# A hybrid layer on one Trainium2 core: weight loads moved to another queue, row statistics split by batch, one Newton step fewer, and the next batch's transposes moved ahead of the output product

## The reference, cut to what matters

```python
def _layernorm(x, axis=-1, eps=1e-05):
    m = jnp.mean(x, axis=axis, keepdims=True)
    v = jnp.var(x, axis=axis, keepdims=True)
    return (x - m) / jnp.sqrt(v + eps)
...
    q = elu(xn @ Wq + bq) + 1; k = elu(xn @ Wk + bk) + 1; v = xn @ Wv + bv      # 16 heads of 16
    kv = jnp.einsum('bkhd,bkhm->bhdm', k, v)
    out = jnp.einsum('bqhd,bhdm->bqhm', q, kv)
    normalizer = jnp.einsum('bqhd,bkhd->bqh', q, k)
    out = out / jnp.maximum(normalizer, 1e-6)[..., None]
    return out.reshape(B, S, D) @ Wo + bo
...
x = x + attention(layernorm(x))      # the layer that the change is about
x = x + ffn(layernorm(x))            # 8 experts, each token goes to one
x = x + mamba(layernorm(x))          # causal convolution, selective scan, gate
x = x + ffn(layernorm(x))
```

## Time and profile before

| what | value |
|---|---|
| median of 3 runs | 1615.09 us (1612.84 to 1615.52) |
| the profiled execution | 1617.17 us |
| its span, first to last instruction | 1615.4 us |
| mean granted TensorE clock | 0.918 of full speed |
| busy: PE, DVE, ACT, POOL | 1385.1, 1063.7, 952.1, 916.6 us |

### The profile page before, as it was taken

The page is one execution under the profiler, slowest core; times in us unless marked ns, Lnnn a source line. Parts: engine busy times, 40 slices in busy tenths (PEclk is TensorE's granted clock), DMA queues, the critical chain, the costliest instruction groups (busy, mean ns, idle before and its releaser), DMA issues.

```text
span 1615.4 us, 22069 instructions
## 1 busy us (share of the span) xinstructions
PE 1385.1 (86%) x6934; PEld 979.2 (61%) x6934; DVE 1063.7 (66%) x1625; ACT 952.1 (59%) x1749; POOL 916.6 (57%) x417
## 2 busy tenths in 40 slices
PE   2899878799997998989989899999997652949997
PEld 1566576799843555555655556555565541938997
DVE  5566546233341798999899998899989983362332
ACT  1222121343324899998998989989899870203442
POOL 1111000455300799889989899898998984004552
PEclk9999968899998999999999999999998685568999
DMA  9100021667430494894958949579496793316663
GB/s 301 50 26 26 27 78 52 206 207 211 117 104 14 100 225 107 194 206 110 223 131 196 221 111 222 139 175 217 101 225 156 161 222 104 126 40 193 207 208 95
DMA packets 98196, 235.66 MB, mean 146 GB/s; under 512 B 10601, under 2 KB 41454, under 8 KB 85552
## 3 DMA queue, kind: packets, MB, share of 16 engines
q0 software_dynamic: 21376, 119.30, 33.8%
q1 hardware_dynamic: 72496, 111.42, 22.7%
q10 hardware_dynamic: 4224, 3.67, 0.7%
HBM read 116.65 MB, written 18.88 MB: 84 GB/s over the span
## 4 chain that ended last, share of the span: by engine, by line
PE 62%; ACT 11%; DVE 11%; issue 8%; POOL 4%; DMA 2%; SPq 1%; ACTq 1%; POOLq 0%; DVEq 0%
PE ps L1110 11%; PE ps L1334 10%; PE ps L1265 9%; PE ps L1274 8%; ACT arena L630 4%; ACT arena L640 4%; PE ps L1363 4%; DVE arena L1058 4%; PE ps L1135 3%; PE ps L1303 3%; POOL arena L423 2%; PE ps L1405 2%; PE ps L1172 2%; PE ps L1126 2%; PE ps L1208 2%
## 5 line engine op out<-in xcount | busy, mean ns | idle before, releaser
L1110 PEld LDWEIGHTS ps<-cst,arena 128*128 128x128 f32 x2524 | 330.8, 152 | 364.0 <-issue 234.2
L423 POOL TENSOR_TENSOR arena<-arena 128x2048 f32<-128x2048 f32 x98 | 463.0, 4726 | 117.9 <-DVE arena L1058 87.9
L1110 PE MATMUL ps<-cst,arena 128*128 128x128 f32 x2524 | 410.2, 293 | 119.4 <-ACT arena L640 49.3
L1058 DVE TENSOR_TENSOR_SCAN arena<-arena,ps 128x512 f32<-128x512 f32 x392 | 471.3, 1212 | 61.7 <-PE ps L1110 53.1
L630 ACT ACTIVATE arena<-arena,a_neg 128x512 f32<-128x512 f32 x512 | 366.5, 716 | 51.6 <-DVE arena L1058 38.7
L640 ACT ACTIVATE arena<-arena,m_bt 128x512 f32<-128x512 f32 x512 | 363.4, 710 | 0.9 <-PE ps L1110 0.9
L1334 PE MATMUL ps<-arena,tapw 128*128 128x512 f32 x512 | 261.0, 609 | 0.0
L392 POOL DMA_INDIRECT arena<-rows,arena x78 | 76.0, 974 | 246.0 <-DVE arena L912 222.5
L932 DVE TENSOR_TENSOR arena<-ps,arena 128x256 f32<-128x256 f32 x78 | 33.2, 425 | 204.0 <-PE ps L1274 141.8
L1265 PEld LDWEIGHTS ps<-arena 128*128 128x128 f32 x1248 | 155.6, 197 | 3.8
L1058 DVE TENSOR_TENSOR_SCAN x<-arena,ps 128x512 f32<-128x512 f32 x120 | 143.8, 1211 | 19.7 <-PE ps L1110 17.8
(11 more groups left out here) (150 smaller groups left out, 1628.5 us busy)
## 6 DMA issues: line engine op xcount, KB each, us to landing
arena<-in_W SPq DMA_DIRECT2D x94, 512.0 KB, 8.9
arena<-arena POOLq DMA_DIRECT2D x45, 1024.0 KB, 8.7
arena<-c_rows SPq DMA_DIRECT2D x128, 256.0 KB, 3.9
x<-arena POOLq DMA_DIRECT2D x29, 1024.0 KB, 8.8
arena<-x POOLq DMA_DIRECT2D x15, 1024.0 KB, 8.9
rows<-x SPq DMA_DIRECT2D x16, 512.0 KB, 3.4
x<-x POOLq DMA_DIRECT2D x7, 1024.0 KB, 9.2
x<-residual SPq DMA_DIRECT2D x12, 512.0 KB, 5.5
```

The costliest lines, as they stand in the source:

```text
L423: g.tensor_tensor(h, h, m_c[i % RC].unsqueeze(1).to_broadcast([P, KI, SEQ]), ALU.mult)\
L1058: v.tensor_tensor_scan(out=h[:, k, :], data0=m_a[g % RA], data1=ps[SCAN_BANK[g % 3]][:, :], initial=0.0, op0=ALU.mult, op1=ALU.add).then_i ...
L1110: return t.transpose(bank, src[:, k * P:(k + 1) * P], ident)
```

## The change

Seven edits in four engines' programs:

1. The loads of x count on three semaphores (batch 0, batch 1, batches 2 to 7) in place of two.
2. The six `ld_m` loads move from ACT's program to SP's, behind `load_ffn`. ACT's wait for all of x goes with them.
3. A Newton step fewer: three in place of four, everywhere.
4. DVE does the statistics and scales of batch 1 alone at the start.
5. DVE waits for the rest of x, and takes the row statistics of chunks 8 to 15 (`EARLY = 8`), between `a_norm(1)` and `a_kvbias(0)`.
6. The row statistics of chunks 16 to 31, and the scales of chunks 8 to 31, stand between `a_kfeature(0)` and `a_mask(0)`.
7. PE does `a_turn(b+1)` before `a_out(b-1)`, in the loop and in every batch that has both.

```diff
+EARLY = 8
...
-                sp.dma_start(x[:, b * CPB:(b + 1) * CPB, :], xin[:, b]).then_inc(S(f"ld_x{min(b, 1)}"), 16)
-            sp.wait_ge(S("ld_x1"), 16 * (BATCH - 1))
+                sp.dma_start(x[:, b * CPB:(b + 1) * CPB, :], xin[:, b]).then_inc(S(f"ld_x{min(b, 2)}"), 16)
+            sp.wait_ge(S("ld_x2"), 16 * (BATCH - 2))
             load_ffn(sp, 0)
+            for dst, name in ((zw, "zw"), (dtw, "dtw"), (bcw, "bcw"), (outw, "outw")):
+                sp.dma_start(dst[:, :, :], T[name].rearrange("(k p) n -> p k n", p=P)).then_inc(S("ld_m"), 16)
+            sp.dma_start(a_neg[:, :, :], T["A_log"]).then_inc(S("ld_m"), 16)
+            sp.dma_start(mvec[:, :, :], T["mvec"]).then_inc(S("ld_m"), 16)
...
-            a.wait_ge(S("ld_x1"), 16 * (BATCH - 1))
-            for dst, name in ((zw, "zw"), (dtw, "dtw"), (bcw, "bcw"), (outw, "outw")):
-                a.dma_start(dst[:, :, :], T[name].rearrange("(k p) n -> p k n", p=P)).then_inc(S("ld_m"), 16)
-            a.dma_start(a_neg[:, :, :], T["A_log"]).then_inc(S("ld_m"), 16)
-            a.dma_start(mvec[:, :, :], T["mvec"]).then_inc(S("ld_m"), 16)
...
-                for _ in range(4):
+                for _ in range(3):
...
-            def first_stats(lo, hi):
+            def first_stats(lo, hi, at=None):
                 for c in range(lo, hi):
                     last = row_stats(c)
                 link(last)
-                layer_norm_scales(lo, hi)
+                layer_norm_scales(lo if at is None else at, hi)
...
                 if before:
                     a_normalise(b - 1)
+                else:
+                    v.wait_ge(S("ld_x2"), 16 * (BATCH - 2))
+                    for c in range(2 * CPB, 2 * CPB + EARLY):
+                        row_stats(c)
                 a_kvbias(b)
                 a_qfeature(b)
                 a_kfeature(b)
+                if not before:
+                    first_stats(2 * CPB + EARLY, NCH, 2 * CPB)
...
-            v.wait_ge(S("ld_x1"), 16 * (BATCH - 1))
-            first_stats(CPB, NCH)
+            v.wait_ge(S("ld_x1"), 16)
+            first_stats(CPB, 2 * CPB)
...
                 if before:
                     a_oturn(b - 1, b)
-                    a_out(b - 1)
                 if more:
                     a_turn(b + 1)
+                if before:
+                    a_out(b - 1)
                 a_kvmm(b)
```

## The result

The changed kernel takes 1601.48 us (median of 8 runs, 1594.12 to 1607.94) against 1615.3 (8 runs, 1612.21 to 1620.13): ratio 0.9914, 95% interval 0.9897 to 0.9931. That is 13.9 us less (10.9 to 16.6); 17.2 was forecast, a time of 1598, with a range of 1593 to 1604. The time lies in that range, but above the 1595.5 to 1600.5 that the forecast gave itself: it falls to the first rival, lost clock (1600.7 to 1605). The profiled execution took 1602.8 us, its span is 1601.0 us.

A forecast was written before the change was run, and what follows sets the result against it. At the start PE was taken to wait for ACT's queue, then to bound the attention loop, with DVE's Newton steps ahead of the feed. Start 14.9 - pause 4.3 + transposes 5.2 + Newton 1.4 = 17.2 us off: 1598, range 1593 to 1604.

The forecast's parts named there:

- the first rival, lost clock: The pause or the feed costs PE clock, +2.7 to +7 us, a time of 1600.7 to 1605; chance 0.20.
- query(0) starts: PE's first query matmul, released by ACT, starts at 16.6 us, 14.9 earlier.
- kvbias(0) starts: DVE's first kvbias is wanted at 24.5 us; eight early statistics end at 24.0, a cover of 0.5.
- pause of PE ahead of attend(0): Inserted statistics and scales delay mask(0), so PE idles 4.3 us, from 39.0 to 43.3.
- attend(0) starts: First attend on PE starts at 43.3 us where it started at 53.94; 10.6 us won.
- clock behind the pause: Slow PE clock after the new pause: 0 in the sum, +2.7 us allowed for in the range.
- moved transposes, six batches: Attention loop: transposes fill 0.87 of PE's 1.25 us hole, in batches 1 to 6; 5.2 us saved.
- Newton step, each feed: DVE's scales ahead of each of the two feeds: one step fewer saves 0.72 us each, sum 1.4.
- the dearer end: At the start, ACT's table load of 1.3 us taken as behind the waits; ahead of them gains 1.3 more.
- The weight loads on SP: Six late loads, 7.6 us on ACT, behind load_ffn on SP: cost nothing, without cover at most 7.6.
- The 2.7: Extra time if PE's new pause brings a slow stretch as long as the first query's, 6.15 us for 3.44.
- another share of slow clock in the feed: Sign that the prediction is wrong: the profile's clock windows show a different slow portion in the feed.

The follow-up runs named there:

- only_turns: Kernel before with one edit: the next batch's transposes stand ahead of the output product; ratio 0.9974 to before.
- undo_turns: Changed kernel with the next batch's transposes back behind the output product; ratio 0.9941 to before.
- newton9: Changed kernel with nine Newton steps in place of three where the scales of all 32 chunks are made, ahead of the two feeds; ratio 0.9943 to before.
- after: First profile of the changed kernel with all seven edits against the kernel before; profiled execution 1602.8 us, span 1601.0 us.
- only_queue: Kernel before with the six late weight loads moved from ACT to SP and ACT's wait for all of x removed; ratio 0.9998 to before.
- fill_hole: Changed kernel with four more 128x512 matmuls, result unused, on PE between the first kvmm and query(1); ratio 0.9899 to before.
- spread: Changed kernel with only the scales of chunks 8 to 15 ahead of mask(0), the other inserted work in DVE's waits of the next two batches; ratio 0.9917.
- spread2: Kernel spread with the scales of chunks 16 to 31 cut in two and placed ahead of the normalisations, where POOL is idle; 1593.33 us, ratio 0.9863 to before.
- before: First profile of the kernel without the change, span 1615.4 us; median time 1615.3 us.

## Why the prediction was right, point by point

The change is faster by what the forecast named, and the steps that the code sets came out to 0.4 us. What the clock sets didn't: it was put at 0 and cost some us, and the time is in the range because the range took in the near part of that rival.

| step | forecast | profile after |
|---|---|---|
| query(0) starts | 16.6 | 16.23 |
| kvbias(0) starts | 24.5 | 24.43 |
| pause of PE ahead of attend(0) | 4.3 | 4.21 |
| attend(0) starts | 43.3 | 43.17 |
| clock behind the pause | 0 (2.7 in the range) | 3.2 (0.3 to 3.2 in six profiles) |
| moved transposes, six batches | 5.2 | 5.2 |
| Newton step, each feed | 0.72 | 0.72 |

**The start.** The table load stands behind the wait, the dearer end, as taken. The transposes ended at 13.6 and released ACT, not the weights; that is the 0.4. **The transposes.** From 66.16 to attend(7) at 183.32 there are 117.2 us where there were 121.5 (74.68 to 196.22), five turns 0.87 shorter, and the sixth lies ahead of them; only_turns and undo_turns agree with 5.2 within their intervals. **Newton steps.** The two feeds' first matmuls stand 0.7 us nearer to what precedes them; newton9 shows 0.71 a step. The first feed's transposes start at 204.66, not at the 201.4 of the forecast: the 3.3 us are the clock behind the pause. **The weight loads on SP** cost nothing that shows: SPq has no share in the chain after.

**The term that was mis-sized** is the clock. The forecast said "I put 0 into the sum". Behind the inserted statistics the six profiles with the pause show 0.3 to 3.2 us, the eight without it nothing at that place. The 2.7 that the text had worked out and put beside the rule was near to the dearest of them. Trainium skill, TensorE: Matmul & The Clock Gate, HAM oscillation — how this bites in real kernels, says that a pause can send TensorE back to its slow clock; the granted clock of 0.65 in 42 to 43, at the end of the pause, agrees with it. The forecast's own signs of being wrong included another share of slow clock in the feed, and this one came: 36.9 us for 31.0 in the first feed of *after*.

The steps as measured make 10.8 (53.94 - 43.17) + 5.2 + 1.4 = 17.4 us, less 1.8 for the mean of the clock behind the pause 15.6. The 10.8 is of two profiles; over three with the old start attend(0) comes at 54.4 in the mean, over five of the changed kernel and its near kin at 42.7, which makes it 11.8 and the sum 16.6. Measured was 13.9 with an interval up to 16.6.

**The rest is clock too.** The mean granted clock of whole executions tells more than the few profiles: 0.9185 over 54 executions of the kernel before, 0.9143 over 14 of the changed one, 0.0042 lower (0.0026 to 0.0058). Some 0.0008 of that is arithmetic, since 15 us in which PE stood at full clock have gone. The other 0.0034 are at most 5.4 us of time, by an estimate that takes PE as busy in all of it at half speed. It is an upper bound, since the mean also counts slow stretches in which PE stands, as in only_queue, with 0.53 in 31 to 42 us, 5.16 of them busy, and 0.9140 in the mean. So the lower clock belongs to the change and isn't chance. The first feed fits: 32.7 us in the mean of the five profiles with the late attend(0), 35.2 in the nine with the early one, while the second feed has 35.7 and 35.5; with these 2.5 us 14.1 would be expected.

**What stays open** is why the earlier start brings slower clock to the first feed, and how much of the lower mean is the pause's: the three kernels with the early start and no pause ahead of attend(0) (fill_hole, spread, spread2) have 0.9158 over 14 executions, between the two. The single profiles differ by such terms in both directions (in *after* the stretch between the feeds took 3.0 us less than in *before* and the second feed 3.1 less, the first 5.9 more), so the 14.4 us between two spans confirm nothing alone.

**What the forecast overlooked** is how much the placement left on the table. It took the pause of 4.3 us for the price of the change; spread2 shows that the pause and the clock behind it together were worth 6.7 us at attend(7), and some 8 in the time (3.6 to 12.9).

## What to carry to other kernels

Two queues that both stand in front of a start have to be cleared together: one edit alone measured 0.9998, the other 1.0032, both together (with the Newton step, in undo_turns) 0.9941. Work that is taken off the start has to be laid into waits that the profile shows, in pieces no longer than these; put as one block behind the next milestone it comes back as a pause of the busiest engine, and in four of six profiles with slow clock behind it. Before a piece is laid into a wait of DVE, look at what POOL does in it.

## What the runs showed of the hardware

**DVE behind POOL.** A DVE instruction of 4 columns took 2.29 us (14.10 to 16.39) beside POOL's addition (14.03 to 16.36), its like 0.17; in spread one of 16 columns 2.26. Row statistics kept their 0.34 us each beside such an addition (in spread seven in 2.38 us from 38.58 on, POOL from 38.86 to 41.22). The Trainium skill, SBUF — State Buffer, Who interferes with whom, says that DVE and GpSimd share a pair of ports that one of them holds for a whole instruction, taken by DVE only in some forms, such as two SBUF inputs, or a tensor_scalar where its operands allow a mode with two ports. The Newton product of two SBUF operands that stood and the statistics with one input that didn't agree with it. The instruction that stood in spread is a tensor_scalar with one input; that it ran in such a mode no run here shows.

**The clock of the feed comes in steps.** 31, 33.8 or 36.9 us for the same instructions in fourteen profiles of kernels that are alike there, and PE at 0.50 to 0.57 for most of the stretch though it is busy for 26.8 of 30 us. Four larger matmuls ahead of it, with 4.55 us between, changed nothing that the time shows.
